# Level sums of a selective scan: three bf16 products on parts made by GpSimd, in place of one fp32 product

## The reference

```python
xz = x @ w_in                                  # xc, z: 256 channels each
xc = silu(causal_dwconv(xc, conv_w))
bc = xc @ w_bc                                 # B_t, C_t: 64 states each
dt = softplus(xc * w_dt + dt_bias)
A = -exp(a_log)
# for every token t:
h = exp(dt_t * A)[..., None] * h + (dt_t * xc_t)[..., None] * B_t[:, None, :]
y_t = einsum('bcn,bn->bc', h, C_t)
# then: (y + d_skip * xc) * silu(z) @ w_out
```

## Time and profile before

| | us |
|---|---|
| runs | 4424.13, 4427.06, 4427.88 |
| median | 4427.06 |
| span of the profiled execution | 4429.7 |
| TensorE busy | 3571.8 (81%) |
| VectorE busy | 3317.4 (75%) |
| ScalarE busy | 2847.9 (64%) |
| GpSimd busy | 971.8 (22%) |
| chain that ended last | PE 43%, DVE 27%, issue 14%, ACT 3% |

### The profile page before, as it was taken

How to read it: one execution, slowest core, us unless ns; L and a number is a source line. 1 busy time by engine, 2 the same in 40 slices (tenths; PEclk the granted TensorE clock), 3 DMA queues, 4 the chain that set the end, 5 groups by cost and what they waited for, 6 DMA issues and landing times.

```text
span 4429.7 us, 73632 instructions
## 1 busy us (share of the span) xinstructions
PE 3571.8 (81%) x28566; PEld 1826.0 (41%) x28566; DVE 3317.4 (75%) x5155; ACT 2847.9 (64%) x4792; POOL 971.8 (22%) x1447
## 2 busy tenths in 40 slices
PE   6999868999899998999996555555555558899998
PEld 4666512222344445676673111111111115566666
DVE  6777767777311127787886999999999996778887
ACT  3655415556344445666665999999998995566665
POOL 2444422100467630000001231222221210000000
PEclk8999859999999999999997555555555559899999
DMA  1000031331511100000001101111101110000000
GB/s 48 1 1 1 1 72 29 57 58 20 115 31 35 31 20 6 12 6 11 2 2 22 22 17 20 22 22 22 22 17 19 22 20 20 6 12 7 7 2 21
DMA packets 256809, 97.45 MB, mean 22 GB/s; under 512 B 223795, under 2 KB 241854, under 8 KB 256446
## 3 DMA queue, kind: packets, MB, share of 16 engines
q1 hardware_dynamic: 256462, 92.74, 10.5%
HBM read 31.75 MB, written 2.23 MB: 8 GB/s over the span
## 4 chain that ended last, share of the span: by engine, by line
PE 43%; DVE 27%; issue 14%; ACT 3%; DMA 1%; POOL 0%; SPq 0%; DVEq 0%; ACTq 0%; POOLq 0%
DVE d_negmax L2820 12%; PE psum L2351 7%; PE psum L2380 6%; DVE f_m_E L2450 6%; PE psum L2366 6%; PE psum L2055 5%; PE psum L2077 5%; PE psum L1443 3%; DVE wl_negmax L1563 2%; PE psum L1432 2%; DVE f_pT_E L2469 2%; PE psum L1420 2%; ACT d_junk L2878 2%; PE psum L2753 1%; PE psum L2742 1%
## 5 line engine op out<-in xcount | busy, mean ns | idle before, releaser
L2820 DVE TENSOR_REDUCE d_negmax<-psum 128x1 f32<-128x1024 f32 x1024 | 1175.6, 1210 | 52.2 <-PE psum L2753 51.1
L2878 ACT ACTIVATE d_junk<-psum,d_negmax 128x1024 bf16<-128x1024 f32 x1024 | 1138.8, 1114 | 103.7 <-DVE d_negmax L2820 95.9
L2753 PE MATMUL psum<-d_qT,d_kT 64*128 64x512 bf16 x2048 | 607.3, 602 | 547.4 <-ACT d_junk L2878 526.5
L2544 ACT ACTIVATE hidden<-psum,f_nm_E 128x1024 f32<-128x1024 f32 x512 | 566.5, 1113 | 144.6 <-DVE f_nm_E L2453 144.5
L2450 DVE TENSOR_REDUCE f_m_E<-psum 128x1 f32<-128x1024 f32 x512 | 601.7, 1216 | 48.1 <-PE psum L2351 47.0
L2753 PEld LDWEIGHTS psum<-d_qT,d_kT 64*128 64x128 bf16 x2048 | 105.8, 101 | 1050.4 <-ACT d_junk L2878 990.0
L2351 PE MATMUL psum<-f_k_E,f_q_swapped_E 64*128 64x512 f32 x1024 | 528.3, 626 | 6.6 <-ACT hidden L2544 6.6
L2351 PE MATMUL psum<-f_k_E,f_q_E 64*128 64x512 f32 x1024 | 528.0, 625 | 2.9 <-DVE f_v_E L2441 1.9
L2380 PE MATMUL psum<-f_pT_E,f_v_E 128*64 128x128 f32 x8192 | 506.3, 277 | 2.5 <-DVE residual L2480 2.5
L2551 ACT COPY f_pT_E<-psum 128x512 f32<-128x512 f32 x512 | 299.9, 586 | 322.3 <-PE psum L2366 322.3
L2469 DVE COPY f_pT_E<-psum 128x512 f32<-128x512 f32 x512 | 351.3, 686 | 161.4 <-PE psum L2366 152.0
(11 more groups left out here) (330 smaller groups left out, 4539.2 us busy)
## 6 DMA issues: line engine op xcount, KB each, us to landing
moe_gates_on_all<-moe_gate_spill SPq DMA_DIRECT2D x16, 1024.0 KB, 11.8
f_q_swapped_E<-f_q_E SPq DMA_DIRECT2D x64, 128.0 KB, 2.3
moe_w<-in_moe_w SPq DMA_DIRECT2D x15, 256.0 KB, 6.5
out<-residual SPq DMA_DIRECT2D x1, 2048.0 KB, 8.7
residual<-in_hidden_states SPq DMA_DIRECT2D x2, 768.0 KB, 7.9
wl_qT<-wl_q_rows SPq DMA_TRANSPOSE x48, 3.3
residual<-in_hidden_states SPq DMA_DIRECT2D x2, 256.0 KB, 3.3
m_taps<-in_m_conv SPq DMA_DIRECT2D x4, 128.0 KB
```

The lines of the kernel that those rows point to most:

```text
L2544: A.activation(pb[:, u % 2, f * 2 * BANK:(f + 1) * 2 * BANK], two(2 * f), ACT.Exp, bias=nm[:, u % 4:u % 4 + 1], scale=SC, accum_out=rs[:, ...
L2753: last = T.matmul(bank(2 + 2 * (at % 3) + jj), kT[half, s, jb * P:(jb + 1) * P], qT[half, s, hf * BANK:(hf + 1) * BANK], start=True, stop= ...
L2820: V.tensor_reduce(mh[:, t % 2, n // 2, n % 2:n % 2 + 1], two(2 + 2 * (at % 3)), X, ALU.max, negate=True).then_inc(*maxed.up(at))
L2878: A.activation(junk[:, at % 3, :], two(2 + 2 * (at % 3)), ACT.Exp, bias=mh[:, t % 2, n // 2, n % 2:n % 2 + 1], accum_out=sh[:, t % 2, n // ...
```

## The change

For quads 1 to 7 GpSimd, behind the scaling, splits `dta` into three bf16 parts: the value rounded, the remainder rounded, and what then remains. The remainder is kept in `wq`, so GpSimd waits for `dtx_done` first. TensorE waits for the new signal `split(q)` and makes, for each mask, three bf16 products that accumulate in the same half bank. The masks are converted to bf16 once, on GpSimd, behind the scaling of quad 0. Steps 0 to 3 keep the fp32 product.

```diff
+                sums_b = sb(st, "level_sums_bf16", [P, 8, P], BF16)
+                dtp = sb(st, "m_dta_parts", [P, 3, SLOTS, DI], BF16)
+                split = signal("m_dta_split", [q for q in qs if q])
+                sums_done = signal("level_sums_done", [0])
@@ def pe_front(i, j):
-                    if j == 0 and i % Q4 == 0:
-                        T.wait_ge(*scaled(i // Q4))
+                    if j == 0 and i == 0:
+                        T.wait_ge(*scaled(0))
+                    elif j == 0 and i % Q4 == 0:
+                        T.wait_ge(*split(i // Q4))
+                        if i == Q4:
+                            T.wait_ge(*sums_done(0))
                     for h in range(2):
-                        last = T.matmul(bank(bd)[:, h * DI:(h + 1) * DI], sums[:, 2 * j + h, :], dta[:, i % SLOTS, :], start=True, stop=True)
+                        o = bank(bd)[:, h * DI:(h + 1) * DI]
+                        if i < Q4:
+                            last = T.matmul(o, sums[:, 2 * j + h, :], dta[:, i % SLOTS, :], start=True, stop=True)
+                            continue
+                        for n in range(3):
+                            last = T.matmul(o, sums_b[:, 2 * j + h, :], dtp[:, n, i % SLOTS, :], start=(n == 0), stop=(n == 2))
                     last.then_inc(*summed.up(i, j))
@@ def dve_rest(q):
                     if q:
-                        V.wait_ge(*scaled(q - 1))
+                        V.wait_ge(*(split(q - 1) if q > 1 else scaled(0)))
@@ def pool_scale(q):
                     G.wait_ge(*dt_done(q))
                     G.tensor_tensor(quad(dta, q), wq[:, :, :], row(neg_a), ALU.mult).then_inc(*scaled.up(q))
+                    if q == 0:
+                        G.tensor_copy(sums_b[:, :, :], sums[:, :, :]).then_inc(*sums_done.up(0))
+                        return
+                    G.wait_ge(*scaled(q))
+                    G.wait_ge(*dtx_done(q))
+                    rem = wq
+                    p3 = [quad(dtp[:, n], q) for n in range(3)]
+                    gstep(G.tensor_copy(p3[0], quad(dta, q)))
+                    gstep(G.tensor_tensor(rem[:, :, :], quad(dta, q), p3[0], ALU.subtract))
+                    gstep(G.tensor_copy(p3[1], rem[:, :, :]))
+                    G.tensor_tensor(p3[2], rem[:, :, :], p3[1], ALU.subtract).then_inc(*split.up(q))
```

## The result

| | before | after |
|---|---|---|
| median of the runs, us | 4425.6 | 4458.9 |
| lowest to highest | 4414.04 to 4427.88 | 4454.8 to 4464.84 |
| span of the profiled execution, us | 4429.7 | 4460.5 |

The ratio after to before is 1.008, with a 95% interval of 1.0064 to 1.0096: slower by 0.8%. The forecast was 4469 us in a range of 4443 to 4492.

A forecast was written before the change was run, and what follows sets the result against it. TensorE was busiest (81% of the span), with GpSimd's chain to its sums lacking room at quads 2, 4, 6 and 7. 4429.7 + 40.5 + 13 - 11.4 = 4471.8, less 2.6 gives 4469 us; range 4443 to 4492.

The forecast's parts named there:

- the wait: TensorE's first sums of quads 1 to 7 wait for GpSimd's split, stalling the whole scan: 40.5 us together.
- the clock: TensorE's granted clock falls to 1.2 GHz behind six stalls, 2.2 us each: 13 us (9 to 17).
- the products: TensorE's level sums in bf16 shorten the front by 0.6 us in 19 steps: 11.4 us gained (2 to 19).
- contention: In GpSimd's split, VectorE instructions with two SBUF operands hold it up: 1.0 us added to 6.7 a split.
- rival C: In the scan, TensorE's clock stays up and the products' gain is whole: 4436 us; chance 0.07.
- Rival A: In TensorE's bf16 sums the weight loads are exposed, 0.49 us against 0.46 for fp32: 4485 us; chance 0.10.
- Dearer split (B): VectorE holds up each of GpSimd's four split instructions by 1 us, 10.7 us a split: 4494 us; chance 0.10.
- faster (D): GpSimd splits within its chain's room; decided at about 3 us a split, 4420 us with 1 us; chance 0.03.

The follow-up runs named there:

- e4: The changed kernel, with TensorE running products that nobody reads ahead of its wait for the split; 4449.1 us, ratio to before 1.0043.
- e2: The changed kernel without the split: bf16 products from constant parts, TensorE waiting for the scaling alone; 4414.8 us, ratio to before 0.9971.
- e1: The changed kernel with fp32 products in all steps, TensorE still waiting for GpSimd's split; 4477.0 us, ratio to before 1.0109.
- e9: The kernel before plus GpSimd's split, whose results nobody reads; fp32 sums wait for the scaling alone; 4439.7 us, ratio to before 1.0037.

## Why the prediction was right, and where not

The direction, the place and the mechanism came as forecast: GpSimd's chain had no room, the split of 6.7 us lies on it, TensorE's queue stands, its clock falls (behind five of the six stalls), the products give back a part. The forecast was 10 us too high (4469 for 4458.9). That it came so near is in part luck: in scan time, which is all that it spoke of, it had 42.1 us for 27.1, and 6.2 us of the measured 33.3 lie outside the scan. Term by term, in scan time:

| term | forecast | measured | by |
|---|---|---|---|
| the wait | +40.5 | +35.2 | 36.5 after against 1.3 before |
| the clock | +13 | +7.7 | e4 against after |
| the products | -11.4 | -14.8 | e2, and its 2.6 of new wait for the scaling |
| sum | +42.1 | +28.1 | scan time +27.1 |

**The wait.** The split itself was right to the tenth: 1.04 + 2.12 + 1.11 + 2.18 and the hand-overs are 6.73 us (179.22 to 185.95), forecast 6.7. The term that was mis-sized here is the 1.0 us a split that I added for contention, 6.7 us over all quads. The earlier trace rows show one instruction of VectorE held up beside GpSimd, and I read them as "hold each other up". That is so where VectorE's begins first, as at the scaling, whose 3.4 us of the earlier trace rows have 1.0 us of it in them (2.35 alone); the four instructions of the split were held up by 0.08 at most. Without that 1.0 my own count is 33.8, beside 35.2 measured in the change and 34.3 in e1 (35.6 less 1.3). The six long stalls were in the right places. Quads 2, 6 and 7 stood 7.54, 7.53 and 7.14 us, forecast about 8; quads 3 and 5 stood 3.81 and 2.95, forecast 4.5. Quad 4 stood 7.53 as well.

**The clock.** The granted clock fell behind five of the six stalls, and rival C, in which it stays up, is false. But 2.2 us each was too much, and this is the other term that was mis-sized. Behind 7.54 us idle the front of step 8 took 4.99 us (186.10 to 191.09) against 3.24 without, a loss of 1.75; in quad 7 it was 2.3. But behind 7.53 us in quads 4 and 6, and 3.81 in quad 3, it was 0.9 to 1.0, and behind 2.95 in quad 5 nothing. The length of the stall alone does not give the loss: in quads 4 and 6 the clock was back before the front was over, and why is not shown. The six make 7.0, and e4 gives 7.7 (9.8 by the medians). I had sized the term from two stalls, of which one showed 1.5 us; adding to it for the other, and taking one size for all six, was the error. The convolution that comes next (L520 at 193.14, 16 records) took 1.95 us, as without a stall, so behind this stall nothing was lost beyond the front.

**The products.** 0.110 us a record came for 0.112, the front takes 3.24 for 3.31, and so gains 0.81. The forecast had 0.74 and cut it to 0.6 for steps in which ScalarE is late anyway. ScalarE was late more often (20.0 us in 23 places, 13.6 in 10 before), but that did not take the gain: 19 x 0.81 is 15.4, near the 14.8 measured. Rival A, which needed 0.163 a record, is false. The bf16 rows told this for 512 columns, and it holds for 256. The Trainium skill (TensorE: Matmul & The Clock Gate, Part 3: Packing small matmuls) lets a load run beside products in flight only if its row group is another; the trace disagrees here too, with 672 records of one full row group at 0.110 us, about half of the 0.215 that 512 columns took the earlier trace rows, so next to nothing of the loads is paid.

**Dearer split (B) and faster (D).** B put the cost of contention on the split in GpSimd's chain, where there is next to none, and D needed a split of about 3 us. What neither of them saw, and my forecast did not either, is that a split off the path still costs 8 to 10 us of scan time. In the change itself this seems to be mostly hidden, as I had argued: TensorE is standing at the time, and the terms without it add up to within 1.0 us.

**The remainder.** The scan's 27.1 us are not the whole of the 33.3 between the medians. 3.8 more of the span lie ahead of and behind the scan, and the rest is within the spread of the runs (13.8 us for the four runs of the kernel before, 10.0 for those of the change).

## What to carry to other kernels

A wait of 0.3 us in the profile is not a small wait, it is an exact fit: whatever lengthens the chain behind it comes through in full, and here 6.7 us of GpSimd work per quad became 7.5 us of standing TensorE in three quads of seven (7.1, 3.8, 3.0 and nothing in the others), against the 3.2 us (4 x 0.81) that the quad's products saved. Ask of every helper what else it slows by merely running: the same work, awaited by nobody, still cost 1.4 us a quad. And where a stall can't be removed, filling it with products that are thrown away kept the clock up and was worth about 8 us of scan time.

## What was not expected of the hardware

- GpSimd and VectorE do not share the loss; the one that began second had it. In the split VectorE's instructions with two operands in SBUF grew from 0.45 to 2.25 us and from 0.42 to 1.14, which is about how long GpSimd's instruction beside them ran (2.12 and 1.11), while GpSimd's grew by 0.08 at most over the time they took alone. At the scaling, where VectorE's L706 had begun first, GpSimd took 3.4 us in place of 2.35. The Trainium skill (GPSIMD Engine Reference, section 1) names the contention with VectorE's instructions of two SBUF inputs; the trace agrees.
- Seven splits that nobody waits for cost 10.0 us of scan time (e9), 1.4 each for 6.7 of work.
- A bf16 record of 256 columns with a weight load of its own follows the one before in 0.110 us, so three of them (0.33) are cheaper than one fp32 product (0.46).
- Stalls of the same length did not cost the same behind them. TensorE stood 7.54, 7.53, 7.53 and 7.14 us in quads 2, 4, 6 and 7, and the front behind lost 1.75, 0.9, 1.0 and 2.3 us; 3.81 us in quad 3 cost 1.0, and behind 2.95 us in quad 5 the clock was still at 2.4 GHz and nothing was lost.
